# Down product of an expert layer with 17 matmuls a tile in place of 18, and a fourth small act product

## What is computed

```
logits = xt @ router_w.T
topk_w, topk_idx = top_k(softmax(logits), 2)
topk_w = topk_w / sum(topk_w)
comb = einsum('tk,tke->te', topk_w, one_hot(topk_idx, 8))
for e in range(8):
    gate = silu(xt @ Wg[e].T)
    up = xt @ Wu[e].T
    out = out + gate * up @ Wd[e].T * comb[:, e:e + 1]
```

## Time and profile before

| | |
|---|---|
| median of three runs | 288.37 us |
| the runs | 287.08, 288.47, 288.37 us |
| the profiled execution | 287.14 us |
| its span, first to last instruction | 285.3 us |
| TensorE busy | 234.7 us, 82% of the span |
| VectorE busy | 172.4 us, 60% |
| ScalarE busy | 151.0 us, 53% |
| GpSimd busy | 135.6 us, 48% |
| granted TensorE clock, mean | 0.896 |

### The profile page before, as it was taken

One profiled execution on the slowest core, in us unless ns is written; L12 is line 12 of the kernel. 1 busy time (PEld: TensorE's weight loads), 2 busy tenths in 40 slices (PEclk: granted clock), 3 DMA queues, 4 the chain that ended last, 5 costly groups with the idle time before them and its releaser, 6 DMA issues.

```text
span 285.3 us, 5001 instructions
## 1 busy us (share of the span) xinstructions
PE 234.7 (82%) x1404; PEld 156.9 (55%) x1405; DVE 172.4 (60%) x419; ACT 151.0 (53%) x275; POOL 135.6 (48%) x180
## 2 busy tenths in 40 slices
PE   1898999497964226699989999998899999999970
PEld 1525667256754213367656656665567766666650
DVE  2248689469789999395765755755744444434420
ACT  2114694587566904486766767765543343334410
POOL 1028669249945018204564564564544454545222
PEclk9999997889575555789999999999999999999995
DMA  7994276607630208847457454322333232233211
GB/s 260 343 412 196 67 239 207 249 2 220 241 110 1 74 0 274 290 148 224 104 163 215 82 153 137 68 32 53 83 52 62 57 59 55 55 55 65 31 19 18
DMA packets 15729, 36.91 MB, mean 129 GB/s; under 512 B 1941, under 2 KB 9493, under 8 KB 15706
## 3 DMA queue, kind: packets, MB, share of 16 engines
q1 hardware_dynamic: 9978, 26.09, 26.5%
q0 software_dynamic: 5152, 9.08, 16.9%
q10 hardware_dynamic: 576, 1.46, 1.4%
HBM read 31.49 MB, written 6.19 MB: 132 GB/s over the span
## 4 chain that ended last, share of the span: by engine, by line
PE 35%; issue 21%; DMA 14%; DVE 14%; POOL 9%; POOLq 2%; ACT 2%; SPq 1%; DVEq 0%
PE bank L689 13%; PE bank L715 8%; DMA out<-shared,dest_i 6%; DMA staged<-in_w 5%; POOL rows L1345 4%; DMA W<-in_wmod 3%; PE bank L526 3%; PE bank L699 2%; PE bank L492 2%; DVE W L958 2%; POOL x L1345 2%; PE bank L572 2%; POOL unscale L1353 1%; POOLq L1351 1%; PE bank L537 1%
## 5 line engine op out<-in xcount | busy, mean ns | idle before, releaser
L689 PE MATMUL bank<-W,x 128*128 x414 | 89.2, 371 | 1.3 <-ACT x L882 0.9
L1379 POOL DMA_INDIRECT out<-shared,dest_i x23 | 36.5, 1587 | 80.2 <-DVE shared L1236 80.2
L689 PEld LDWEIGHTS bank<-W,x 128*128 128x128 f16 x414 | 41.2, 100 | 43.5 <-issue 6.2
L1226 DVE SCALAR_TENSOR_TENSOR shared<-bank,unscale,x 128x256 f32<-128x256 f32 (+1 forms) x69 | 28.1, 456 | 48.0 <-ACT x L888 48.0
L888 ACT ACTIVATE x<-bank,unscale 128x256 f32<-128x256 f32 (+1 forms) x69 | 27.1, 455 | 49.6 <-POOL unscale L1353 38.5
L715 PE MATMUL bank<-W,shared 128*128 x414 | 51.0, 276 | 2.2 <-DVE shared L1249 1.7
L715 PEld LDWEIGHTS bank<-W,shared 128*128 128x128 f16 x414 | 39.7, 99 | 8.7 <-issue 2.9
L763 ACT ACTIVATE W<-staged,w_scale_bits 128x1408 f16<-128x1408 f32 (+1 forms) x24 | 35.9, 1500 | 13.0 <-DVE w_scale_bits L947 11.2
L958 DVE SCALAR_TENSOR_TENSOR W<-staged,w_scale_bits,W 128x1408 f16<-128x1408 f32 (+1 forms) x24 | 41.7, 1746 | 0.2
L756 ACT ACTIVATE W<-staged 128x1408 bf16<-128x1408 f32 (+1 forms) x24 | 33.9, 1413 | 11.8 <-DMA staged<-in_w 11.8
L1249 DVE TENSOR_TENSOR shared<-bank,shared 128x512 f16<-128x512 f32 (+1 forms) x46 | 23.5, 552 | 15.0 <-ACT shared L897 15.0
(11 more groups left out here) (179 smaller groups left out, 310.4 us busy)
## 6 DMA issues: line engine op xcount, KB each, us to landing
staged<-in_w SPq DMA_DIRECT2D x16, 704.0 KB, 5.7
staged<-in_w SPq DMA_DIRECT2D x8, 768.0 KB, 4.3
token_rows<-mod_rows SPq DMA_DIRECT2D x4, 259.0 KB, 10.4
x<-in_x SPq DMA_DIRECT2D x4, 256.0 KB, 9.3
W<-in_wmod SPq DMA_DIRECT2D x2, 512.0 KB, 8.9
W<-mod_rows SPq DMA_DIRECT2D x4, 256.0 KB, 4.5
out<-x SPq DMA_DIRECT2D x4, 256.0 KB, 4.2
token_rows<-rows SPq DMA_DIRECT2D x4, 256.0 KB, 3.1
```

What stands on the lines that cost most here:

```text
L689: mm = pe.matmul(bank[2 + n][:, 0:2 * w], half[:, kc * P:(kc + 1) * P], W1_pairs[:, bass.ds(e * 2 + part, 1), :, kc, n * PIECE:n * PIECE + w],
L1226: ve.scalar_tensor_tensor(act[:, n * PIECE:n * PIECE + w], bank[2 + n][:, w:2 * w], unscale[c % 2][:, 1:2], sig[:, n * PIECE:n * PIECE + w ...
L1379: po.indirect_dma_start(out, bass.IndirectOffsetOnAxis(dest_i[:, j:j + 1], 0), y_sb[r], None, bounds_check=last_row, oob_is_err=True, comp ...
```

## The change

The last 64 neurons now stand twice in the sixth chunk, in the activations and in the weights, so that the chunk has 128 rows. In the high half of the down matrix the lower 64 partitions of the chunk hold the high half of these neurons' weights, and the upper 64 their low half. So the product high by high of this chunk holds high by low too, and the sixth matmul of high by low goes. In the third product the chunk adds low by low as well.

```
-LAST_FROM = F - P
+FULL = F // P
+HALF = F - FULL * P
...
+NTH2 = {e: 1 + [prep for prep in PREPARED if prep[1] == W2_OF].index((e, W2_OF)) for e in range(E)}
...
-    gap = np.zeros((FC * P - F, D), np.float32)
     at = (FC - 1) * P
-    down = [by_partition(np.concatenate([Wd[e].T[:at], gap, Wd[e].T[at:]], axis=0)) for e in range(E)]
+    down = [by_partition(np.concatenate([Wd[e].T[:at], Wd[e].T[at:], Wd[e].T[at:]], axis=0)) for e in range(E)]
...
             def turn_act(i, c):
-                pe.wait_ge(s["act_ok"], len(PIECES) * (4 * i + c + 1))
+                pe.wait_ge(s["act_ok"], (len(PIECES) + 1) * (4 * i + c + 1))
                 for fc in range(FC):
-                    at = min(fc * P, LAST_FROM)
                     bk, col = (bank[5], fc * P) if fc < 4 else (bank[6], (fc - 4) * P)
-                    mm = pe.transpose(bk[:, col:col + P], act[:, at:at + P], keep[:, C_ID:C_ID + P])
+                    mm = pe.transpose(bk[:, col:col + P], act[:, fc * P:(fc + 1) * P], keep[:, C_ID:C_ID + P])
...
-                terms = [(a, fc, part) for a, part in ((act_hi, 0), (act_hi, 1), (act_lo, 0)) for fc in range(FC)]
-                for k, (a, fc, part) in enumerate(terms):
+                terms = [(act_hi, 0, fc) for fc in range(FC)] + [(act_hi, 1, fc) for fc in range(FULL)]
+                terms += [(act_lo, 0, fc) for fc in range(FC)]
+                for k, (a, part, fc) in enumerate(terms):
...
                 n = UNIT[e, m]
                 ve.wait_ge(s["hi_ok"], n + 1)
-                ve.scalar_tensor_tensor(unit_out(W1_16, W2_16, e, m, 1), staged[n % STAGED][:, 0:unit_cols(m)], scale_of(e, m),
-                                        unit_out(W1_16, W2_16, e, m, 0), ALU.mult, ALU.subtract).then_inc(s["lo_ok"], 1)
+                high, to, cols = unit_out(W1_16, W2_16, e, m, 0), unit_out(W1_16, W2_16, e, m, 1), W1_MAT if m < 2 else FULL * D
+                if m == 2:
+                    ve.scalar_tensor_tensor(high[HALF:P, cols:], staged[n % STAGED][HALF:P, cols:W2_EXP], scale_of(e, m)[HALF:P, :],
+                                            high[HALF:P, cols:], ALU.mult, ALU.subtract).then_inc(s["tail_ok"], 1)
+                    ve.wait_ge(s["tail_ok"], NTH2[e])
+                ve.scalar_tensor_tensor(to[:, 0:cols], staged[n % STAGED][:, 0:cols], scale_of(e, m),
+                                        high[:, 0:cols], ALU.mult, ALU.subtract).then_inc(s["lo_ok"], 1)
...
+                ve.scalar_tensor_tensor(act[:, F:F + HALF], bank[2 + n][:, 2 * w - HALF:2 * w], unscale[c % 2][:, 1:2],
+                                        sig[:, F - HALF:F], ALU.mult, ALU.mult).then_inc(s["act_ok"], 1)
```

More of the change, by code:

```diff
@@ L233, in layer @@
         y_sb = [shared[:, r * D:(r + 1) * D] for r in range(2)]
-        act = shared[:, 2 * D:2 * D + F]
-        act_hi = shared[:, 2 * D + F:2 * D + F + FC * P // 2].bitcast(F16)
-        act_lo = shared[:, 2 * D + F + FC * P // 2:2 * D + F + FC * P].bitcast(F16)
+        act = shared[:, 2 * D:2 * D + FC * P]
+        act_hi = shared[:, 2 * D + FC * P:2 * D + 3 * FC * P // 2].bitcast(F16)
+        act_lo = shared[:, 2 * D + 3 * FC * P // 2:2 * D + 2 * FC * P].bitcast(F16)
         xs = [rows1[:, r * ROW_ALL:(r + 1) * ROW_ALL] for r in range(2)] + [x[:, r * ROW_ALL:(r + 1) * ROW_ALL] for r in range(2)]
@@ L323, in layer @@
             expo_ok sub_ok sel_ok sums_ok cnt_done tile_ok order_ok tokens_ok place_ok table_done source_ok dest_ok wt_ok wt_done weights_ok
-            sumsq_ok norm_done wscale_ok hi_ok lo_ok
+            sumsq_ok norm_done wscale_ok hi_ok tail_ok lo_ok
             gu_done sig_ok act_ok xt_done slot_ok slot_weight_ok unscale_ok at_done act_hi_ok act_lo_ok down_done y_ok""".split()
```

## The result

The changed kernel takes 293.41 us (median of six runs, 291.62 to 294.61) against 288.42 us (286.83 to 290.85) for the kernel before in the same session. The ratio is 1.016, with an interval of 1.010 to 1.023, so the change costs about 4.7 us (2.9 to 6.5). The direction was forecast; the size, +2.5 us and 290.9 us, was not: the result lies 0.4 us above the range.

What follows compares the result with a forecast made beforehand. A ring through VectorE, GpSimd and ScalarE was taken to bound tiles 4 to 12, TensorE tiles 13 to 22. Act products 2.28 + splits 0.96 + routing 0.25 - late gains 1.02 = +2.5 us, so 290.9 us; range 287.4 to 293.0.

Steps and rivals of the forecast that it cites:

- The bound: Loop of tiles: tiles 4 to 12 bound by the ring, 7.40 us each; tiles 13 to 22 by TensorE, 6.50 us each.
- the ring: Tiles 4 to 12: result, GpSimd's scatter, gather and unscale, ScalarE's sigmoids, VectorE's act products, next result; each waits for the previous.
- its term: Fourth act product on VectorE: 0.19 us a tile, 2.28 us for tiles 0 to 11.
- One, at 86.86 ...: 0.25 us on the path: Split low product at the head of VectorE's routing: delays arithmetic that ends with GpSimd's product, 0.25 us.
- rival B: Routing: GpSimd's product gets between the two low products, 0.6 us over the forecast, 291.5 us; chance 0.13.
- A wait in one gives the next one room, and half of it counts: Tiles 12 to 22: of a 0.13 us wait of the transposes half counts; tiles gain 0.05 or 0.11 us each.
- the room at the transposes' load: Tile 18: the transposes' weight load had 0.17 us to spare after the act products' end.
- Four ... release the unscale ...: 4 x 0.24: Split low products of tiles 2, 5, 8 and 11 delay the unscale or down product: 0.24 us each, 0.96 us.
- the first window: From gate and up of tile 4 to that of tile 13: grows from 66.6 to about 69.0 us.
- the term of 0.17 us: Last down product, after everything else: 0.17 us of its 3.11 us go with the matmul removed.
- both unknown prices at their high ends: Upper bound, whole kernel: act product at 0.27 us and low product split at 0.39 us, +4.4 us.
- D: All 23 tiles: TensorE sets them and each gains 0.11 us, 2.5 us faster, 285.9 us; chance 0.11.

Runs made afterwards that it cites:

- e9: Kernel before, with GpSimd's unscale of tile j + 2 computed ahead of its wait for tile j's result; 278.32 us, ratio 0.972.
- e2: Kernel before, with only the fourth act product and the wider act added, still 18 matmuls; 289.58 us, ratio 1.012.
- e8: Changed kernel, without VectorE's wait between the small and the wide low product; 292.41 us, ratio 1.021.
- e13: e10 with the wide low product ahead of the small one; 278.21 us, ratio 0.978.
- e3: Kernel before, with only the low product of the down matrix split in two; 288.85 us, ratio 1.006.
- e5: Changed kernel, with TensorE's load of the next tile's expert number moved ahead of the wait for the act products; median 294.14 us, ratio 1.015.
- e10: Changed kernel, with GpSimd's unscale of tile j + 2 computed ahead of its wait for tile j's result; 277.02 us, ratio 0.967.
- e1: Kernel before, with only one matmul removed, 17 instead of 18; 286.28 us, ratio 0.9996.
- e6: Kernel before, with the result put ahead of the low product of the step, from tile 2 on; median 285.42 us, no ratio.
- e4: Changed kernel, with the low product of expert 1's down matrix left in one piece; 291.02 us, ratio 1.014.

## Why the prediction was right in direction and wrong in size

**The bound and the ring: right.** The ring closes through VectorE's queue, and e9 shows it by opening it. The act product added cost what its term says, 0.19 us a tile, in the changed kernel's rows and in eight of e2's nine tiles. The estimate from the fixed term of the Trainium skill ("VectorE: DVE Perf Modes", section on the TRN2 errata) was 0.14 us a tile; the rows say 0.19.

**"One, at 86.86 ...: 0.25 us on the path": wrong, 0.95 us** (1.21 at the first maximum). This is the first step that failed. I had the mechanism as rival B and gave it 0.13, because "0.05 us either way undo it". That was wrong twice. The coincidence is no chance: GpSimd's product starts 0.48 us after VectorE's low product in before (86.86 and 87.34 in the earlier trace rows), in after (88.16 and 88.64), in e8 and in e13, since both follow the same work on VectorE, and the small product lasts just that long. And a GpSimd product that comes too early for the boundary only waits for it, as in e13, where it came 1.1 us early and still went ahead of the second piece. It got in in all five profiles with the small piece in front (after, e3, e5, e8, e10). The rival's price for this place, 0.25 + 0.6 = 0.85 us, came near the 0.95 measured, but not by its own steps: the arithmetic that was to find GpSimd free waited again (0.79 us), because the second GpSimd product runs beside the wide one as well, and L1136 gave time back. That row's 0.43 us, taken in the prediction as what such a piece may cost, was itself a wait for GpSimd.

**"A wait in one gives the next one room, and half of it counts", -0.85 us: wrong, +0.36 us.** This is the second step that failed, and it weighs more. I measured the room at the transposes' load, 0.17 us. What matters is when gate and up can start, and that was 1.03 us after the last act product in tile 18 already, without any wait of the transposes that the waits name. There was no room: the ring's pace for a pair of tiles (12.82 us in e1) was TensorE's (12.82 in e9). So the product's 0.19 us came in where the matmul's 0.11 should have gone: e2 lost 0.74 us there, e1 gained 0.55 instead of 1.1. The register load behind the wait is 0.3 us of the distance in the loop's tiles (e5); putting it ahead got back 0.66 us of the ten tiles, in one profile. With the ring open (e9, e10) the change gains 1.05 us there.

**"Four ... release the unscale ...: 4 x 0.24": the path right, the size too small.** A split in the ring costs 0.36 us, since the small piece doesn't overlap its predecessor as the whole product did. In e3 the splits cost 0.34 + 0.96 = 1.30 us where 0.96 were forecast, and in e2 the act products 0.35 + 1.53 = 1.88 us where 2.28 were. The two errors are opposite, so the sum for the ring, 0.72 + 2.47 = 3.19 us in after against 2.28 + 0.96 = 3.24, and the 69.2 us of the first window against 69.0, came out by luck.

**The sum.** For all but the last down product, whose clock differs too much to read the term of 0.17 us, the forecast was 2.28 + 0.96 + 0.25 - 0.85 = 2.64 us and the stretches give 4.50: 0.70 more in the routing, 1.21 more in the late tiles, 0.05 less in the ring. The range's end, 293.0 us, took in both unknown prices at their high ends (+4.4 us), but no place where a gain turns into a loss, and rival B's extra came on top of the forecast alone.

**The rival on the other side.** D, faster by one matmul a tile, was wrong for this kernel. With the ring open its mechanism shows in the last ten tiles, 0.105 us each in e10 against e9.

## What to carry to other kernels

Before sparing TensorE a matmul, look whether the stretch belongs to TensorE. Where a ring through a slow engine's wait sets the time, the spared matmul is worth nothing and every VectorE instruction added to the ring costs its whole spacing; here moving GpSimd's small product ahead of its long wait was worth 7.5 us, the change itself minus 4.7. And a VectorE instruction in two pieces can cost more than its start: at the boundary GpSimd work that has been waiting got in, so look at what GpSimd has ready beside it, not at whether the times coincide. Room on TensorE is read from the instruction that has to start in the end, with the register loads ahead of it.

## What the hardware showed unexpectedly

- At the routing GpSimd's product got in at the first boundary between the two pieces of the low product in all seven profiles that have one there. The boundary is 0.03 us wide, with a semaphore between the pieces or without. The loser pays nearly in full: 1.55 became 2.57 us, 0.48 became 1.38, and GpSimd's 128x512 product 2.20 or 2.39 instead of 1.26.
- A small VectorE product of 64 partitions (64x256) starts 0.03 us behind its predecessor, where the whole 128x1536 product started 0.08 us before its predecessor's end (in the ring; e3 and before).
- The issue of an indirect DMA on GpSimd lengthens behind the start of a long VectorE instruction: the scatter 1.58 to 2.77 us beside L958 in e6, and gathers 1.08 to 2.46. The Trainium skill ("SBUF — State Buffer", section "Who interferes with whom") infers for a tensor_tensor, with two inputs there and no two-port mode, that it takes only the read side and leaves this issue alone. For the SCALAR_TENSOR_TENSOR here, which has two inputs there too, the trace shows the issue lengthened; no run here tests the tensor_tensor itself.
- In tile 18, in the loop, gate and up started 1.01 to 1.07 us behind the last act product with the register load behind the wait (before, after, e2, e4, e8), and 0.77 us with it ahead (e5). In the written-out tiles it was 0.83 and 0.77 us.
- Kernels with the same instructions up to the routing differed by 4.3 us there from execution to execution, and by 1.7 us in tile 1. A single pair of profiles is to be read by stretches that repeat, not by its totals.
